# A two-layer decoder in one program: another cycle for the routing steps, another order at the first expert, and the mixers' first loads moved

## The chip, the cores and the metric

The kernel runs on one core of a Trainium2 chip. The metric is the device time of one execution in microseconds (us): the median of three runs was 3338.87 us (3336.57 to 3339.21). The profile is one execution more, and took 3336.63 us.

## The reference

The reference is a decoder of two layers with residual sums, on x of 8 sequences x 256 tokens x 512, all in float32. Each of its six blocks is fed the layer norm of x. Layer 0: causal attention with rotary positions, 16 heads and a window of 64; masked cross-attention to a context, with a layer norm of its own; then the mixture of experts that this change is about. Layer 1: a state-space mixer (Mamba2 form, chunks of 64), a channel attention to the context, and a feed-forward block of eight LoRA experts.

```python
logits = x @ gate_weight.T                       # x: 2048 tokens x 512, 64 experts
scores = softmax(logits)
gidx = top_k(scores.reshape(T, 8, 8).max(-1), 3)       # 3 of 8 groups
topk_w, topk_i = top_k(where(group mask, scores, 0), 6)    # 6 of 64 experts
pos = cumsum(one_hot(topk_i.flat)) at the chosen expert - 1     # place in the expert's list
slot = topk_i.flat * 192 + minimum(pos, 191)           # 192 slots per expert
buf = zeros(64 * 192, 512); buf[slot] = x[tok]
out = (silu(buf @ Wg.T) * (buf @ Wu.T)) @ Wd.T         # per expert, 704 wide
y = sum over 6 of out[slot] * topk_w
shared = silu(x @ Sg.T) * (x @ Su.T) @ Sd.T            # 704 wide
x = x + y + shared
```

The places in an expert's list run through all 2048 tokens in order, so the slots of a sequence need the counts of all sequences before it.

## The kernel before, in words

The program is a row of stages. In a stage each engine has its own instruction list, written out by hand in a `nc.Block()`: TensorE (`pe`), VectorE (`dve`), ScalarE (`act`), GpSimd (`pool`) and SyncE (`sp`), which issues most of the DMAs. They are ordered by counting semaphores alone (`wait_ge`, `then_inc`), and an engine executes its list strictly in order. At the end of a stage SP waits for all engines to be done (L145; each drains its queue at L129, GpSimd through `pool_link`) before the next stage's semaphores are used. Products in float32 are made of three products of a high and a low part (`..._hi`, `..._lo`): ScalarE writes the high part, VectorE or GpSimd subtracts it to get the low one.

The stages by the trace: attention up to about 821 us, the shared expert with the routing up to 1101, the 64 experts up to about 1904, the mixers of layer 1 up to about 2660, the LoRA experts to the end.

**Shared expert and routing** (`shared_expert`). The work is cut into 48 chunks g: 8 sequences s times six slices n of the 704 columns (`CHUNKS = NM * nseq`, `s, n = divmod(g, NM)`). In step g TensorE does `gate_up(g)` (L1175, three products of gate and of up for the slice), then `down(g - 2)` (L1190). ScalarE makes the tanh of the gate, VectorE the product `sact` (`gated`, `act_lo`), so a chunk's `down` comes two steps behind. After the last slice of a sequence VectorE adds the residual (`out`, `so`) and SP stores it as `mid`.

Between these products stands the routing of sequence r. Its steps and engines:

- `turn_rows(r, j)` on TensorE, for the two tiles j of 128 tokens; ScalarE's `turned` writes `h32` and `hT2`'s high part, GpSimd's `rows_lo` the low one (before: in slices 0 and 1 of sequence r - 1).
- `router(r)` on TensorE (L188, 64 columns of logits in PSUM bank 0), in slice 3 of sequence r - 1 (`router_step`), ahead of that step's `down`. It waits for `slot_ready` of sequence r - 1, since bank 0 also holds the counts and places.
- `negmax`, `exponentials` and `groups` in slice 4, `experts(r)` in slice 5 (VectorE, with ScalarE's exp; ends in `sel`, L1300).
- `counts(r)` on TensorE (L1153): the running counts as a product with a triangular matrix, in slice 0 of sequence r itself (`counts_step`), waits for `sel_ready`.
- `slots_of_experts(r)` and `slots(r)` on VectorE (`slots_steps`), in slices 1 and 2; for sequences 1 and 0, where the counts come in slice 1 or 2, both in one slice. They end in `slot_r` (L1326) and `tok_f` (L1327). SP stores weights and slots as `route_w` and `slots`.
- twelve scatters on GpSimd (L1042), from slice 3 on, two per slice, four per slice for the last sequence: each writes the token numbers of 128 slots to `slot_token`. `pool.wait_ge(sy["act_sh_ready"], g)` keeps them with the chunks.

For the last sequence `turn_last` and one reduction find the last token of each expert (slot 191); SP stores it. At the end of SP's list stand the waits for `so_out` of both buffers (one semaphore for `route_w`, `slots` and `mid`) and for the scatters.

**Experts.** Per expert SP loads indices and weights, GpSimd gathers 192 rows in two DMAs (`xg`, L1463), TensorE turns them (`turn_rows`, L1545), ScalarE copies them out (`xT_copy`, L1481) and VectorE makes the low part (`xT_lo`, L1605); then come the gate and up products (L1560), the activation on ScalarE and VectorE (L1500, L1633) and the `down` products. ScalarE's `hi_gu` and `hi_down` (L1490) and VectorE's `lo_gu` and `lo_down` split the weights. Ahead of the loop (`quads`) the first expert's list is written out: ScalarE does `hi_gu(0, 0)`, eight pad copies into the tails of `wd2` and `aT2` (L1520 to L1527, `epad_ready`), `hi_down(0, 0)`, `xT_copy(0, 0)`, `hi_gu(0, 1)`. TensorE waits for `ezero_ready` and for all eight pads, then turns the rows. VectorE does `lo_gu` twice, `lo_down` twice, then `xT_lo`. At the end of its list SP issues the loads of the mixers' weights (`next_weights`, semaphore `w3_in`): `w_in`, `small` and `w_mo`.

**Mixers.** For sequence s GpSimd gathers, in twelve indirect DMAs (`gather`, L1832), the experts' output rows into `yk`; VectorE adds them weighted to `xn` (`combine`, then the layer norm's statistics `mv`, L2278, and GpSimd's `norm`, L174), and TensorE turns the rows. `xn` (four buffers) is `mid`. SP's list begins with the loads of the routes of two sequences, of their `mid` rows, of the context and of two more sequences of `mid`; GpSimd waits for `routes_in` before its first gather, and its gathers of sequence 1 wait until VectorE has used the rows of sequence 0 (`yk_used`). VectorE does `combined_norm(0)` first, then the constants of the stage (`w3_in`, `norm_w`), then the loop over pairs of sequences.

Of the kernel before, what the change touches and what calls it, by code (L numbers as in the profile page):

```python
# [37 lines left out]
P = 128  # L38
# [48 lines left out]
hr_in0 hr_in1 xr_in0 xr_in1 so_out0 so_out1  # L87
# [836 lines left out]
def shared_expert(nc, sy, const, dr, held, nseq=NSEQ):  # L924
# [5 lines left out]
    with ExitStack() as ctx:  # L930
# [15 lines left out]
        hT2 = [parts(f"hrT{b}", [P, KC, S]) for b in range(2)]  # L946
# [34 lines left out]
        def counts_step(s):  # L981
            return max(0, 2 - s)

        def slots_steps(s):
            return (counts_step(s) + 1, max(2, counts_step(s) + 1))

        def router_step(s):
            return 4 if s == 0 else 3
# [9 lines left out]
        def _(sp):  # L998
# [9 lines left out]
            load_resid(1)  # L1008
            for s in range(nseq):
# [4 lines left out]
                sp.dma_start(dr["route_w"][s], etop[s % 2][:]).then_inc(sy[f"so_out{s % 2}"], 16)  # L1014
                sp.wait_ge(sy["slot_ready"], s + 1)
                sp.dma_start(dr["slots"][s], slot_r[s % 2][:]).then_inc(sy[f"so_out{s % 2}"], 16)
# [5 lines left out]
                sp.wait_ge(sy["shared_ready"], NT * (s + 1))  # L1022
                sp.dma_start(dr["mid"][s], o[s % 2][:]).then_inc(sy[f"so_out{s % 2}"], 16)
                if s + 2 < nseq:
                    load_resid(s + 2)
            for b in range(2):
                sp.wait_ge(sy[f"so_out{b}"], nseq // 2 * 48)
# [4 lines left out]
        def _(pool):  # L1032
            def rows_lo(s, j):
                pool.wait_ge(sy["hThi_ready"], NT * s + j + 1)
                cols = slice(j * P, (j + 1) * P)
                pool.tensor_tensor(hT2[s % 2][1][:, :, cols], h32[s % 2][:, :, cols],
                                   hT2[s % 2][0][:, :, cols].bitcast(F32), ALU.subtract).then_inc(sy["hTlo_ready"], 1)
# [27 lines left out]
            for g in range(CHUNKS):  # L1065
                s, n = divmod(g, NM)
                if n < NT and s + 1 < nseq:
                    rows_lo(s + 1, n)
                of = s if n >= 3 else s - 1
                if of >= 0:  # L1070
                    if n == 3:
                        pool.wait_ge(sy["slot_ready"], s + 1)
                    pool.wait_ge(sy["act_sh_ready"], g)
                    per = 4 if of == nseq - 1 else 2
                    for i in range(per):
                        scatter(of, per * (g - NM * of - 3) + i)
# [2036 lines left out]
```

## Time and profile before

| | |
|---|---|
| median of three runs | 3338.87 us (3336.57 to 3339.21) |
| the profiled execution | 3336.63 us |
| its span in the trace | 3334.9 us |
| mean granted clock of TensorE | 0.962 |

```profile
PE 3063.9 (92%) x22897; PEld 2472.5 (74%) x22897; DVE 2314.5 (69%) x4413; ACT 1598.0 (48%) x3648; POOL 805.0 (24%) x1000
PE   7999999997899699999999769889899889999999
PEclk9999999998999799999999979999999989999999
DMA  6324233321021677777777521311120032222222
```

The first line is the busy time of each engine, its share of the span and the number of its instructions: PE is TensorE's matmuls, PEld its loads of weights, DVE VectorE, ACT ScalarE, POOL GpSimd. The others cut the span into 40 slices of 83 us: busy tenths of TensorE, the clock granted to it in tenths of full speed, and how busy the DMA engines were. TensorE is nearly full everywhere but at the seams between the stages: slice 14 holds the seam ahead of the experts, slices 23 and 24 that ahead of the mixers.

### The profile page before, as it was taken

How to read it: one execution, taken by the hardware profiler on the slowest of the kernel's cores; microseconds unless marked ns; L12 is line 12 of the kernel's file. 1: busy time of each engine (PE TensorE's matmuls, PEld its weight loads, DVE VectorE, ACT ScalarE, POOL GpSimd, SP SyncE). 2: the span in 40 equal slices, each digit the busy share in tenths (PEclk: the TensorE clock that was granted, in tenths of full speed). 3: DMA queues.
4: the chain of work that ended last, by engine and by line, in shares of the span. 5: the costliest groups of instructions: out<-in, count | busy, mean ns of one | idle time of the engine just before them, and what ended most of it. 6: DMA issues, size and time to landing. Idle time of an engine off the chain costs nothing. (4 is left out here: it accounts for less than half of the span.)

```text
span 3334.9 us, 61560 instructions
## 1 busy us (share of the span) xinstructions
PE 3063.9 (92%) x22897; PEld 2472.5 (74%) x22897; DVE 2314.5 (69%) x4413; ACT 1598.0 (48%) x3648; POOL 805.0 (24%) x1000
## 2 busy tenths in 40 slices
PE   7999999997899699999999769889899889999999
PEld 5666666664888588888888646657576678888888
DVE  4655665564666588888888566868686767777776
ACT  3323333332221455555555336656575655555555
POOL 1221122121445211111111143432323012222222
PEclk9999999998999799999999979999999989999999
DMA  6324233321021677777777521311120032222222
GB/s 260 127 98 148 105 127 104 112 102 39 20 58 40 205 244 242 242 243 240 243 246 248 216 77 58 93 60 56 30 70 7 35 116 79 70 74 73 73 71 70
DMA packets 145099, 401.95 MB, mean 121 GB/s; under 512 B 39200, under 2 KB 48032, under 8 KB 131952
## 3 DMA queue, kind: packets, MB, share of 16 engines
q1 hardware_dynamic: 106448, 323.37, 28.6%
q0 software_dynamic: 18976, 50.45, 5.1%
q10 hardware_dynamic: 19456, 25.18, 2.2%
q8 instruction: 141, 2.31, 0.3%
q14 instruction: 78, 0.64, 0.1%
HBM read 344.16 MB, written 54.76 MB: 120 GB/s over the span
## 5 line engine op out<-in xcount | busy, mean ns | idle before, releaser
L1463 POOL DMA_INDIRECT xg<-normed_rows,idx x128 | 127.8, 998 | 643.3 <-PE psum L1545 589.5
L2631 POOL TENSOR_TENSOR mixf<-act 128x256 f32<-128x256 f32 x128 | 143.7, 1122 | 496.7 <-DVE act L2892 496.7
L174 POOL TENSOR_SCALAR ve<-mv 128x1 f32<-128x1 f32 x112 | 34.9, 312 | 841.6 <-DVE mv L780 575.0
L1560 PE MATMUL psum<-xT_hi,wgu_hi 128*128 128x192 f32 (+1 forms) x1536 | 228.4, 271 | 2.4 <-DVE xT_lo L1605 2.4
L1560 PE MATMUL psum<-xT_lo,wgu_hi 128*128 128x192 f32 (+1 forms) x1536 | 223.3, 268 | 0.0
L1560 PE MATMUL psum<-xT_hi,wgu_lo 128*128 128x192 f32 (+1 forms) x1536 | 222.5, 267 | 0.0
L1599 DVE TENSOR_TENSOR wgu_lo<-wgu,wgu_hi 128x1408 fp32r<-128x1408 f32 x128 | 202.6, 1624 | 22.9 <-ACT wgu_hi L1487 22.7
L1560 PEld LDWEIGHTS psum<-xT_hi,wgu_hi 128*128 128x128 f32 (+1 forms) x1536 | 190.6, 182 | 27.0 <-ACT wgu_hi L1487 21.6
L1500 ACT ACTIVATE eth<-psum 128x192 f32<-128x192 f32 (+1 forms) x192 | 63.4, 330 | 301.0 <-PE psum L1560 301.0
L2002 ACT ACTIVATE scratch<-psum,smin 128x512 f32<-128x512 f32 x256 | 173.9, 686 | 62.5 <-DVE smin L2392 60.3
L1560 PEld LDWEIGHTS psum<-xT_lo,wgu_hi 128*128 128x128 f32 (+1 forms) x1536 | 190.8, 183 | 0.0
L1560 PEld LDWEIGHTS psum<-xT_hi,wgu_lo 128*128 128x128 f32 (+1 forms) x1536 | 190.3, 182 | 0.0
L1487 ACT ACTIVATE wgu_hi<-wgu 128x1408 fp32r<-128x1408 f32 x128 | 169.6, 1382 | 27.1 <-DMA wd<-in_w_d_dram 27.1
L2392 DVE TENSOR_REDUCE smin<-psum 128x2 f32<-128x1024 f32 x128 | 155.3, 1216 | 34.1 <-PE psum L2156 33.3
L2892 DVE TENSOR_TENSOR act<-act,maskT 128x512 f32<-128x512 f32 x128 | 88.1, 689 | 117.7 <-ACT act L2669 117.6
L2166 PEld LDWEIGHTS psum<-ident,scratch 128*128 128x128 f32 x1024 | 108.9, 141 | 59.4 <-issue 38.2
L2166 PE MATMUL psum<-ident,scratch 128*128 128x128 f32 x1024 | 144.8, 281 | 8.1 <-DVE scratch L2399 4.9
L1633 DVE SCALAR_TENSOR_TENSOR eact<-eth,psum 128x192 f32<-128x192 f32 (+1 forms) x192 | 67.6, 352 | 110.8 <-ACT eth L1500 108.9
L2902 DVE TENSOR_TENSOR ca_lo<-act,ca_hi 128x512 fp32r<-128x512 f32 x128 | 134.4, 1050 | 12.5
L558 PE MATMUL psum<-hT_hi,w_slot 128*128 128x256 f32 x768 | 113.1, 291 | 12.2 <-ACT hT_hi L468 5.8
L1042 POOL DMA_INDIRECT slot_token<-tok_i,slot_w x96 | 99.4, 1035 | 80.4 <-DVE slot_r L1326 31.1
L902 DVE TENSOR_SCALAR arena<-psum,hi 128x512 f32<-128x512 f32 x128 | 87.2, 744 | 43.8 <-PE psum L672 43.8
(427 smaller groups left out, 8665.0 us busy)
## 6 DMA issues: line engine op xcount, KB each, us to landing
wgu<-in_w_gu_dram SPq DMA_DIRECT2D x64, 1408.0 KB, 6.1
w_slot<-w_split SPq DMA_DIRECT2D x21, 2048.0 KB, 8.8
wd<-in_w_d_dram SPq DMA_DIRECT2D x64, 512.0 KB, 8.7
w_raw<-in_w_dram SPq DMA_DIRECT2D x128, 256.0 KB, 2.6
expert_out<-yo ACTq DMA_DIRECT2D x64, 256.0 KB, 5.2
w_slot<-w_split SPq DMA_DIRECT2D x28, 512.0 KB, 5.1
wd<-in_w_d_dram SPq DMA_DIRECT2D x64, 192.0 KB, 9.1
w_split<-w_slot SPq DMA_DIRECT2D x4, 2048.0 KB, 9.5
```

Source lines behind the costliest of these rows:

```text
L558: ins = pe.matmul(out, lhs_of(lp, kc), rhs_of(rp, kc), start=(m == 0 and kc == 0), stop=(m == 2 and kc == KC - 1))
L1042: pool.indirect_dma_start(out=dr["slot_token"], out_offset=bass.IndirectOffsetOnAxis(ap=slot_w[s % 2][:, j, k:k + 1], axis=0), in_=tok_i[s ...
L1463: pool.indirect_dma_start(out=xg[b][0:w, t, :], out_offset=None, in_=rows, in_offset=bass.IndirectOffsetOnAxis(ap=idx[b][0:w, t:t + 1], ax ...
L1487: act.activation(wgu2[b][0][:, gu], wgu[b][:, gu], ACT.Copy).then_inc(sy["wgu_hi"], 1)
L1560: ins = pe.matmul(bank(2 + m)[0:w, gu * CAP:(gu + 1) * CAP], wgu2[b][wp][:, gu, kc, m0:m0 + w], xT2[b][xp][:, kc, :], start=(i == 0 and kc ...
L1599: dve.tensor_tensor(wgu2[b][1][:, gu], wgu[b][:, gu], wgu2[b][0][:, gu].bitcast(F32), ALU.subtract).then_inc(sy["wgu_lo"], 1)
L2002: act.activation(prob[:, q % 4, k, :], bank_pair(2 * (q % 2))[:, k, :], ACT.Exp, bias=smin[b][:, n, k:k + 1], scale=-1.0, accum_out=ssum[b ...
L2166: ins = pe.transpose(bank(4 + k)[:, mc * P:(mc + 1) * P], prob[:, q % 4, k, mc * P:(mc + 1) * P], ident)
L2392: dve.tensor_reduce(smin[(q // PAIRS) % 2][:, q % PAIRS, :], bank_pair(2 * (q % 2)), AX.X, ALU.min).then_inc(sy["smin_ready"], 1)
L2631: pool.tensor_tensor(mixf[:, g % LAG, :], act2[:, g % LAG, 0, :], act2[:, g % LAG, 1, :], ALU.add).then_inc(sy["f_mix"], 1)
L2892: dve.tensor_tensor(act2[:, g % LAG], act2[:, g % LAG], maskT[(g // FC) % 2][:, 2:4, :], ALU.mult).then_inc(sy["f_ca"], 1)
L2902: dve.tensor_tensor(ca2[1][:, g % LAG], act2[:, g % LAG], ca2[0][:, g % LAG].bitcast(F32), ALU.subtract).then_inc(sy["f_ca_lo"], 1)
```

## The change

The routing runs in a cycle of its own, of five chunks in place of six (`CYCLE = 5`), so it gets ahead of the chunks of its sequence: rows of sequence r are turned in chunks 5r - 4 and 5r - 3, `router(r)` stands in chunk 5r - 1 behind that chunk's `down`, `negmax` to `groups` in 5r, `experts` in 5r + 1, `counts` in 5r + 2, `slots_of_experts` and `slots` together in 5r + 3, and the twelve scatters in 5r + 4 to 5r + 7, three in each. The turned rows get a third buffer, the stores of routes a semaphore apart from `so_out` (`rt_out`), and SP stores `mid` one turn later. In the experts' stage the first `xT_copy` goes ahead of the pads, the first `turn_rows` ahead of the wait for them, and `xT_lo` ahead of `lo_down`. The mixers' first two routes and first four sequences of `mid` are loaded behind the mixers' weights at the end of the experts' list of SP; the gathers of sequence 1 go to `scratch` and `y[1]`, with semaphores of their own, and wait for nothing; GpSimd's `norm(0)` stands behind 18 gathers; and VectorE's `combined_norm(0)` behind the constants.

```diff
+        CYCLE = 5
+        def in_cycle(g, phase, first=0):
+            r, at = divmod(g - phase, CYCLE)
+            return r if at == 0 and first <= r < nseq else None
+        def turned_in_chunk(g):
+            for j in range(NT):
+                r = in_cycle(g, j - CYCLE + 1, 1)
+                if r is not None:
+                    return r, j
+            return None
...
-        hT2 = [parts(f"hrT{b}", [P, KC, S]) for b in range(2)]
+        hT2 = [parts(f"hrT{b}", [P, KC, S]) for b in range(3)]
...
@@ SP: route_w and slots go to rt_out, mid one turn later
-                sp.wait_ge(sy["shared_ready"], NT * (s + 1))
-                sp.dma_start(dr["mid"][s], o[s % 2][:]).then_inc(sy[f"so_out{s % 2}"], 16)
-                if s + 2 < nseq:
-                    load_resid(s + 2)
+                if s >= 1:
+                    store_rows(s - 1)
+            store_rows(nseq - 1)
...
@@ GpSimd
-                if n < NT and s + 1 < nseq:
-                    rows_lo(s + 1, n)
-                of = s if n >= 3 else s - 1
-                if of >= 0:
-                    if n == 3:
-                        pool.wait_ge(sy["slot_ready"], s + 1)
-                    pool.wait_ge(sy["act_sh_ready"], g)
-                    per = 4 if of == nseq - 1 else 2
-                    for i in range(per):
-                        scatter(of, per * (g - NM * of - 3) + i)
+                if turned_in_chunk(g):
+                    rows_lo(*turned_in_chunk(g))
+                for i in range(4):
+                    r = in_cycle(g, 4 + i)
+                    if r is not None:
+                        pool.wait_ge(sy["slot_ready"], r + 1)
+                        pool.wait_ge(sy["act_sh_ready"], g)
+                        for k in range(3):
+                            scatter(r, 3 * i + k)
...
@@ TensorE
-                if s + 1 < nseq:
-                    if n < NT:
-                        turn_rows(s + 1, n)
-                    if n == router_step(s):
-                        router(s + 1)
+                if turned_in_chunk(g):
+                    turn_rows(*turned_in_chunk(g))
                 if g >= 2:
                     down(g - 2)
-                if s < nseq and n == counts_step(s):
-                    counts(s)
-                if s == nseq - 1 and n == 3:
+                r = in_cycle(g, -1, 1)
+                if r is not None:
+                    router(r)
+                r = in_cycle(g, 2)
+                if r is not None:
+                    counts(r)
+                if g == CYCLE * nseq:
                     turn_last()
...
@@ VectorE: negmax and groups at in_cycle(g, 0), experts at in_cycle(g, 1)
-                if s < nseq and n == slots_steps(s)[0]:
-                    slots_of_experts(s)
-                if s < nseq and n == slots_steps(s)[1]:
-                    slots(s)
+                r = in_cycle(g, 3)
+                if r is not None:
+                    slots_of_experts(r)
+                    slots(r)
...
@@ experts, ScalarE
             hi_gu(0, 0)
+            xT_copy(0, 0)
             act.wait_ge(sy["ezero_ready"], 7)
...
             hi_down(0, 0)
-            xT_copy(0, 0)
             hi_gu(0, 1)
...
@@ experts, TensorE
+            turn_rows(0, 0, 0, True)
             pe.wait_ge(sy["epad_ready"], 8)
-            turn_rows(0, 0, 0, True)
...
@@ experts, VectorE
+            xT_lo(0, 0)
             for part in range(2):
                 lo_down(0, 0, part, 0)
-            xT_lo(0, 0)
...
@@ mixers' tiles and loads
+    for b in range(2):
+        loads += [(tiles[f"slots{b}"][:], dr["slots"][b]), (tiles[f"wk{b}"][:], dr["route_w"][b])]
+    for s in range(4):
+        loads.append((tiles[f"xn{s}"][:], dr["mid"][s]))
...
@@ mixers, SP
-            load_routes(0)
-            load_rows(0)
-            load_routes(1)
-            load_rows(1)
             load_cx(0)
-            load_rows(2)
-            load_rows(3)
...
@@ mixers, GpSimd
-                if n == 0:
-                    pool.wait_ge(sy["routes_in"], 64 * (s // 2 + 1))
-                if s and k == 0:
+                if n == 0 and s < 2:
+                    pool.wait_ge(sy["w3_in"], W3A)
+                elif n == 0:
+                    pool.wait_ge(sy["routes_in"], 64 * (s // 2))
+                if s >= 2 and k == 0:
                     pool.wait_ge(sy["yk_used"], GATHERS * (s - 1) + TOPK * (j + 1))
...
-            for s in range(2):
-                for n in range(GATHERS):
-                    gather(s, n)
-                norm(s, norm1(s))
+            for n in range(2 * GATHERS):
+                gather(n // GATHERS, n % GATHERS)
+                if n == GATHERS + TOPK - 1:
+                    norm(0, norm1(0))
+            norm(1, norm1(1))
...
@@ mixers, VectorE
-            combined_norm(0)
             dve.wait_ge(sy["w3_in"], W3A)
...
+            combined_norm(0)
```

## Rows read from the trace of the kernel before

**Rows 1.** Stretch, length; busy PE, PEld, DVE, ACT, POOL; granted clock; DMA share; GB/s.

```profile
829.00:1088.40 259.40, 244.64 (x1691) 225.16 (x1690) 168.57 (x483) 60.21 (x168) 125.30 (x115) 0.96 0.14 38
1088.40:1101.70 13.30, 0.08 (x1) 0.00 (x0) 0.81 (x2) 0.00 (x0) 2.77 (x3) 0.55 0.11 40
1101.70:1122.70 21.00, 1.94 (x8) 1.57 (x8) 9.06 (x14) 9.74 (x16) 6.20 (x5) 0.50 0.74 244
1122.70:1899.60 776.90, 776.41 (x6456) 687.25 (x6456) 627.02 (x1146) 423.84 (x695) 121.59 (x123) 1.00 0.73 241
1899.60:1935.00 35.40, 0.00 (x0) 0.00 (x0) 11.11 (x17) 1.08 (x3) 14.63 (x21) 0.53 0.58 205
```

**Rows 2.** Waits of TensorE, 820 to 1090 us: total us, times, longest.

```profile
PE psum L188 <- DVE slot_r L1326: 11.8, 7, 3.2
...
PE psum L1153 <- DVE sel L1300: 2.1, 1, 2.1
```

**Rows 3.** Timeline of TensorE, 849 to 857 us: start, duration, instruction, [idle before].

```profile
849.22 0.40 PE L1190 MATMUL psum<-sd_hi,sact_hi 128*128 128x512 f32 x1
...
850.61 0.64 PE L1175 MATMUL psum<-hrT_hi,sg_hi 128*128 128x256 f32 x4
...
853.00 0.64 PE L1175 MATMUL psum<-hrT_hi,su_lo 128*128 128x256 f32 x4
...
856.80 3.01 PE L188 MATMUL psum<-w_gate,hrT 128*128 128x64 f32 x16 [3.16 <-DVE slot_r L1326]
```

**Rows 4.** Timeline of VectorE at the end of the slots of sequence 0.

```profile
856.48 0.17 DVE L1326 CAST slot_r<-over 128x16 int32<-128x16 f32 x1
```

**Rows 5.** Busy time by stretch, behind the wait for `sel` and behind the first for `slot_r`.

```profile
845.00:853.00 8.00, 7.87 (x60) 7.62 (x61) 7.34 (x18) 0.69 (x2) 3.50 (x3) 1.00 0.01 2
857.00:865.00 8.00, 8.00 (x38) 7.31 (x38) 1.46 (x5) 0.70 (x4) 5.91 (x6) 0.57 0.03 1
```

**Rows 6.** Attention stage: a wait of TensorE on the timeline, and that stretch's busy time.

```profile
38.62 3.53 PE L558 MATMUL psum<-w_slot,hT_hi 128*128 128x512 f32 x8 [2.70 <-DVE w_slot L823]
...
38.00:42.00 4.00, 3.38 (x9) 2.68 (x10) 0.56 (x1) 0.00 (x0) 0.00 (x0) 0.57 0.98 416
```

**Rows 7.** End of the shared expert's stage: SP's waits, the drains (ns, starts), the last scatter.

```profile
SPq L145 <- POOLq L129: 9.0, 1, 9.0
...
SPq L145 <- DMA mid<-so: 2.3, 1, 2.3
...
L129 POOLq DRAIN  x2: 679/4331/7983, 815.5 to 1093.0; - x2
...
1090.80 0.98 POOL L1042 DMA_INDIRECT slot_token<-tok_i,slot_w  x1 [0.30 <-issue]
```

**Rows 8.** First expert: timeline of three engines, and a DMA issued at 1106.44.

```profile
1115.10 0.63 ACT L1524 ACTIVATE wd_hi<-wd 32x512 fp32r<-32x512 f32 x1
...
1118.31 1.06 ACT L1490 ACTIVATE wd_hi<-wd 128x1024 fp32r<-128x1024 f32 x1
...
1118.38 1.94 PE L1545 MATMUL psum<-ident,xg 128*128 128x128 f32 x8 [29.91 <-ACT aT_lo L1526]
...
1120.36 0.87 ACT L1481 ACTIVATE xT_hi<-psum 128x384 fp32r<-128x384 f32 x2 [0.48 <-PE psum L1545]
...
1128.15 0.35 DVE L1633 SCALAR_TENSOR_TENSOR eact<-eth,psum 128x192 f32<-128x192 f32 x1 [2.42 <-ACT eth L1500]
...
xg<-normed_rows,idx POOLq DMA_INDIRECT x1, 9.8
```

**Rows 9.** Mixers' start: a load issued at 1862 us, and GpSimd's timeline.

```profile
w_mo<-in_w_mo_dram SPq DMA_DIRECT2D x1, 1024.0 KB, 17.8
...
1909.98 0.96 POOL L1832 DMA_INDIRECT yk<-expert_out,slots  x1 [4.42 <-DMA wk<-route_w]
...
1923.86 1.28 POOL L1832 DMA_INDIRECT yk<-expert_out,slots  x1 [0.30 <-issue]
...
1933.41 0.24 POOL L174 TENSOR_SCALAR ve<-mv 128x1 f32<-128x1 f32 x1 [8.27 <-DVE mv L2278]
```

## What the change will do to the time

> **What bounds the kernel now.** I read the table of stages first [rows 1]: it gives the busy time of each engine in each stretch. In the shared expert's stage TensorE is busy for 244.6 of 259.4 us, and in the experts' stage for 776.4 of 776.9 us, so there only TensorE's own waits and its clock can be saved. Between the stages stand stretches in which TensorE does almost nothing: 13.3 us after the shared expert, 21.0 us ahead of the first expert's products (1.9 us busy), and 35.4 us ahead of the mixers. The change touches the shared expert's stage and all three of these stretches. Next come the waits of TensorE in that stage [rows 2]: 11.8 us in seven waits of the router product for `slot_ready`, and one of 2.1 us for `sel_ready`. Then each such place in order of time [rows 3 to 9]. The chain of waits says little here, since it ends long after.
>
> The change has four parts on the path. Call them A (routing cycle), B (end of that stage), C (first expert) and D (start of the mixers).
>
> **A. Routing in a cycle of five chunks.** A chunk on TensorE is `gate_up` and `down`. From the starts in [rows 3] `down` takes 850.61 - 849.22 = 1.39 us, `gate_up` from 850.61 to 853.64, some 3.0 us there and 2.87 us at its usual pace (24 matmuls at the same spacing of 0.12 us). The work of TensorE is the same as before: no product is added or taken away. What changes is where `router(r)` stands. For r = 1 and 2 VectorE did all of `slots_of_experts` and `slots` in one chunk's step already, and TensorE waited 3.16 us for it [rows 3]; a second such wait of 3.17 us follows 32 us later. For r = 3 to 7 the two halves lay in two steps, and each wait was (11.8 - 2 x 3.16) / 5 = 1.1 us [rows 2]. After the change all seven have the one-step form of r = 1, but `router` comes behind `down(g - 2)`, not ahead of it. TensorE thus arrives 1.39 us later, and the wait is 3.16 - 1.39 = 1.77 us. VectorE's side stays: the `slot_r` that releases it starts at 856.48 [rows 4], 7.3 us after the `gate_up` of that chunk ended, against 1.39 + 3.03 + 1.39 = 5.8 us on TensorE. Waits: 7 x 1.77 = 12.4 us instead of 11.8, so +0.6 us.
>
> The larger item is the clock. After the wait of 3.16 us the granted clock falls from full speed (2.4 GHz) to half (1.2 GHz): its mean over the next eight microseconds is 0.57 [rows 5], a loss of 8 x 0.43 = 3.4 us, and the second wait of this length costs the same 3.4 us. The five waits of 1.1 us are followed by none. The nearest row to a wait of 1.77 us is the one of 2.1 us for `sel_ready` [rows 2], which ends at 845.1 and is followed by a clock of 1.00 [rows 5]; the nearest on the other side is 2.70 us in the attention stage, where the mean is 0.57 over four microseconds [rows 6]. I take no fall at 1.77 us: -6.9 us. Bounds of A: -8.0 (waits 0.2 us shorter) and, if all seven waits cost a fall, +17.5. Taken: +0.6 - 6.9 = -6.3 us.
>
> What else A moves: `turn_rows(1, 0)` leaves chunk 0 for chunk 1, and `turn_rows(1, 1)` goes from 1 to 2; both starts of weights and VectorE hide it. `experts(r)` ends 5.3 us after its `gate_up`, and `counts(r)` comes 1.39 + 2.87 + 1.39 = 5.65 us after it and 1.0 more where two turns lie between: no wait, though with 0.4 us to spare for r = 7. Without that cover it costs up to 0.5 us each. GpSimd gets 12 scatters at 1.27 us and two `rows_lo` at 1.3 us in four chunks, 17.9 us of some 22. On SP's queue the store of `mid` moves one turn back; its buffers are wanted over five chunks later, so it costs nothing. The third `hT2` is what lets the rows be turned early.
>
> **B. End of the stage.** Before, the routing of the last sequence came in chunks 42 to 44 and its twelve scatters lie past the last product: the last starts at 1090.80, GpSimd's DRAIN starts at 1093.0 and takes 7.98 us, and SP waits 9.0 us for it after the store of `mid` has landed (2.3 us) [rows 7]. Afterwards the slots are ready in chunk 38 and the scatters go in chunks 39 to 42. Chunks 43 to 47 and the two last `down` are some 5 x 4.27 + 2 x 1.39 = 24 us, so scatters and drain (1.0 + 8.0 us, and landing) end ahead of the last product. What is late next is the store of `mid`, unchanged. Gain: the 9.0 us. Bounds: -9.5 and 0 (the drain may belong to the stage's end and not to the scatters).
>
> **C. First expert's rows ahead of the pads.** This looks like a gain of the 3.2 us that the eight pad copies take (1115.10 to 1118.31), since TensorE turns the rows at 1118.38, right behind them [rows 8]. But it is one queue: ScalarE now waits for the turned rows before it writes the pads. The second half of the rows is asked for at 1106.44 and takes 9.8 us [rows 8], so it lands at 1116.2; turning takes 2.0 us (to 1118.3), `xT_copy` 0.87 us, the pads 3.2 us: 1122.4. `pe.wait_ge(epad_ready, 8)` still stands ahead of all products, so the first product starts at 1122.4 instead of 1122.73. `hi_down` (1.6 us) follows, to 1124.0, `lo_down` on VectorE (1.9 us) to 1125.9 and `lo_gu(1)` (3.15 us) to 1129.1. Before, VectorE gated the first product at 1128.15 [rows 8]. It is 1.0 us later now and has no slack there: TensorE ends that expert 0.8 us later. The steady state is TensorE's, so this stays. C: +0.8 us. Bounds: -2.0 (rows land 3 us sooner) and +2.5 (rows land 2 us later).
>
> **D. Start of the mixers.** The routes and four sequences of `mid` are loaded by SP behind the mixers' weights, in the experts' stage. That is 2.1 MB in eight more issues at 1862 us; the last weights land 17.8 us after their issue [rows 9], at about 1880, and the mixers start at 1904, so the loads are hidden with some 15 us to spare. GpSimd waited 4.42 us for the routes until 1909.98 [rows 9]; it now goes on at 1905.6. The twelve gathers are a row of 1.26 us each, the last starts at 1923.86, and VectorE works on the second tile as they land; everything up to the first turned rows at 1935 hangs on them. So -4.4 us. Moving VectorE's constants ahead of `combined_norm(0)` fills idle time, and where they stood (3.4 us) VectorE waited 2.2 us more for TensorE: nothing. The twelve gathers of sequence 1 no longer wait for `yk`, but sequence 1 is combined only behind `convolved(0)`, at 1958: nothing either. Behind six of them GpSimd's norm of sequence 0 is now queued. It would be reached at 1905.6 + 18 x 1.26 = 1928.3, and is wanted at 1933.41 - 4.4 = 1929.0 [rows 9]: 0.7 us to spare. Bounds: -5.4 (less traffic beside the gathers) and -1.9. The lower gain is that of gathers as slow as the last one of before, 1.28 us instead of 0.95 [rows 9], for eight or ten of the eighteen.
>
> The Trainium skill has a rule for this in "SBUF — State Buffer", section "Who interferes with whom": a VectorE instruction with two SBUF inputs contends with GpSimd instructions that read SBUF, and the later one waits. The combine is such an instruction, and the last gather's 1.28 us agrees in direction, at 0.33 us and not a whole instruction.
>
> **Sum.** -6.3 - 9.0 + 0.8 - 4.4 = -18.9 us. The profiled execution took 3336.63 us and so would take 3317.7. The median of the runs shown lies 2.2 us above it, so I predict 3320.0 us.
>
> **Rivals.**
> 1. *The clock falls at every router wait* (the other side). Place: TensorE ahead of `router(r)`, seven times. VectorE's one-step routing makes each wait 2.7 us rather than 1.77, and each pays the fall of a long wait. Price: 7 x 2.7 - 11.8 = +7.1, 7 x 3.4 - 6.9 = +16.9, A = +24.0 and the sum +11.4: 3350.3 us, slower. It decides from somewhere between 2.1 and 2.7 us of idle time. For it: one of the five VectorE steps might be longer by 0.4 us. Against it: the 2.1 us row. Chance 0.07.
> The Trainium skill, "TensorE: Matmul & The Clock Gate", section "HAM oscillation — how this bites in real kernels", says that a loop with an idle gap in each turn pays the slow clock in each turn; its gap is longer than the 1.77 us here, and the rows with 2.1 and 3.16 us fit it.
> 2. *The drain isn't hidden*: it is a property of leaving the stage after many scatters. For it: at the end of the attention stage, with no scatters, it takes 0.68 us [rows 7], which fits both readings. B = 0: 3329.0 us. Chance 0.12.
> 3. *The mixers' lead is lost* to GpSimd's queue. D = -1.9: 3322.5 us. Chance 0.11.
> 4. *Two falls of the clock stay*, since the wait of 2.1 us comes just before. A = +0.6: 3326.9 us. Chance 0.08.
> My forecast has the remaining 0.62.
>
> **Numbers.** The range is 3315.5 to 3330.5 us: from the upper gains of B, C and D (-22.3, less 1 us of spread) to rival 2 with a little loss beside it. Some 0.2% (6.7 us) is what a measurement of this kernel can tell from no change. Rival 1 is slower by 0.34%. Everything else is faster by more than 0.2%, less some chance that two rivals meet. Faster 0.88, same 0.05, slower 0.07.
>
> **What would show it.** A: seven waits of 1.6 to 2.1 us of the router product for `slot_r`, and a granted clock of 1.00 from 850 us on to the end of the stage. B: SP's wait for GpSimd's drain is gone, and the next stage starts 3 us after the last `so`. C: ScalarE idle some 3 us ahead of `xT_hi`; first product 0 to 0.5 us earlier and the steady state 0.8 us later, each counted from the stage's start. D: first gather within 2 us of the mixers' start, first turned rows 26.7 us after it instead of 31.0. It would be wrong if a clock below 1 follows the waits, or if the drain stands in the same place.

## The result, and the profile after

The changed kernel takes 3333.51 us (median of 22 runs, 3323.48 to 3337.58) where the kernel before takes 3338.39 us (22 runs, 3334.75 to 3343.21): a ratio of 0.9984, with an interval of 0.9978 to 0.9990. That is 4.9 us, where 18.9 us were forecast, and the time lies outside the range. Forecast faster, it is faster by less than the 0.2% that I had called telling.

The stages after, in the order and the columns of [rows 1]:

```profile
830.03:1093.25 263.22, 247.94 (x1691) 228.44 (x1690) 172.03 (x483) 60.05 (x168) 129.64 (x117) 0.95 0.14 38
1093.25:1097.78 4.53, 0.00 (x1) 0.00 (x0) 0.73 (x2) 0.00 (x0) 0.00 (x0) 0.62 0.29 116
1097.78:1119.09 21.31, 1.94 (x8) 1.57 (x8) 7.30 (x11) 6.72 (x13) 5.34 (x5) 0.50 0.73 240
1119.09:1897.10 778.01, 777.35 (x6456) 688.14 (x6456) 628.44 (x1148) 426.62 (x699) 120.04 (x124) 1.00 0.73 243
1897.10:1929.50 32.40, 0.00 (x1) 0.03 (x1) 14.18 (x25) 0.97 (x3) 22.46 (x27) 0.54 0.68 204
```

The seam behind the shared expert has shrunk from 13.3 to 4.5 us, the one ahead of the mixers by 3 us (the first stretch in which TensorE does nothing there is 32.6 us where it was 35.4). But the shared expert's stage has not. From its first turned rows to its last product it took 266.85 us before (821.63 to 1088.48) and takes 270.59 now (822.66 to 1093.25). The two profiled executions, whose spans differ by 4.6 us (3334.9 and 3330.3), add up as follows:

| part | forecast | measured | from |
|---|---|---|---|
| ahead of the stage, untouched | 0 | +1.0 | 821.63, 822.66 |
| A, first turned rows to last product | -6.3 | +3.7 | 266.85, 270.59 |
| B, last product to next stage's first load | -9.0 | -8.7 | 13.24, 4.53 |
| C, that load to the mixers' start | +0.8 | +1.3 | 802.29, 803.58 |
| D, mixers' start to first turned rows | -4.4 | -2.9 | 31.03, 28.14 |
| behind the mixers' first turned rows, untouched | 0 | +0.9 | 1399.9, 1400.8 |

So 10.0 us are missing in A and 1.5 us in D. In A it is not the waits. TensorE's waits in the stage after, as in [rows 2]:

```profile
PE psum L188 <- DVE slot_r L1337: 12.6, 7, 2.0
PE psum L1163 <- DVE sel L1311: 2.1, 1, 2.1
```

Seven waits, 12.6 us, where 12.4 were forecast. The clock makes the difference. Here are the seven waits on TensorE's timeline, and under them, in the same order, the busy table from each wait's start to nine microseconds behind its end; the granted clock is the third number from the right:

```profile
857.45 1.94 PE L188 MATMUL psum<-w_gate,hrT 128*128 128x64 f32 x14 [1.87 <-DVE slot_r L1337]
886.42 1.75 PE L188 MATMUL psum<-w_gate,hrT 128*128 128x64 f32 x14 [1.87 <-DVE slot_r L1337]
913.42 1.75 PE L188 MATMUL psum<-w_gate,hrT 128*128 128x64 f32 x14 [1.47 <-DVE slot_r L1337]
940.44 2.92 PE L188 MATMUL psum<-w_gate,hrT 128*128 128x64 f32 x14 [1.65 <-DVE slot_r L1337]
970.52 1.90 PE L188 MATMUL psum<-w_gate,hrT 128*128 128x64 f32 x12 [1.88 <-DVE slot_r L1337]
1001.12 2.21 PE L188 MATMUL psum<-w_gate,hrT 128*128 128x64 f32 x14 [2.00 <-DVE slot_r L1337]
1030.24 1.97 PE L188 MATMUL psum<-w_gate,hrT 128*128 128x64 f32 x16 [1.88 <-DVE slot_r L1337]
```

```profile
855.58:866.45 10.87, 9.00 (x60) 8.77 (x60) 5.61 (x21) 1.39 (x6) 6.20 (x6) 0.84 0.16 49
884.55:895.42 10.87, 9.00 (x72) 8.72 (x73) 6.61 (x28) 1.39 (x6) 5.83 (x6) 1.00 0.47 148
911.95:922.42 10.47, 9.00 (x71) 8.78 (x72) 7.42 (x30) 1.39 (x6) 5.80 (x6) 1.00 0.55 151
938.79:949.44 10.65, 9.00 (x46) 8.83 (x47) 5.04 (x16) 1.39 (x6) 5.83 (x6) 0.68 0.53 145
968.64:979.52 10.88, 9.00 (x45) 8.63 (x46) 3.82 (x14) 1.39 (x6) 5.82 (x6) 0.69 0.02 1
999.12:1010.12 11.00, 9.00 (x59) 8.78 (x59) 5.33 (x20) 1.38 (x6) 5.90 (x6) 0.84 0.03 3
1028.36:1039.24 10.88, 9.01 (x72) 8.77 (x72) 6.78 (x28) 1.38 (x6) 6.52 (x7) 1.00 0.02 1
```

Behind waits 1, 4, 5 and 6 the clock falls to half (1.2 GHz) for some time. Length times (1 - clock) is what it costs: 1.7, 3.4, 3.4 and 1.8 us, 10.3 together, against 6.8 us before (two falls of 3.4 us; the first is in [rows 5]). The forecast had put it at nothing. Busy time alone misleads here: TensorE is busy for all nine microseconds either way, but it gets through 46 matmuls in one stretch and 72 in another.

### The profile page after: what moved, and what is told of

It is laid out like the page before. It is cut to its first block and busy times, and to the rows that moved or that the text cites. A ratio compares the mean times of both kernels' runs of the same rounds, so it can differ in the third digit from the quotient of the medians.

```text
span 3330.3 us, 61582 instructions
## 1 busy us (share of the span) xinstructions
PE 3071.3 (92%) x22897; PEld 2479.2 (74%) x22897; DVE 2317.9 (70%) x4413; ACT 1596.5 (48%) x3648; POOL 805.7 (24%) x1000
```

## The experiments

Each kernel was run beside the kernel before, which took 3377.36 us in the first set of runs (e1 to e4), 3376.91 in the second (e5 to e8), 3338.03 in the third (e9 to e12), 3378.09 in the fourth (e13 to e15) and 3380.59 in the last. Where it is near 3378 the mixers' stage, which lies behind all that is studied here, takes 31 to 48 us more in the traces; so each time is read against the before of its own set, and each part from its own stretch of the trace. "Stage" is first turned rows to last product of the shared expert's stage, "clock" what slow clock costs in it from 834 us on; a "fall" is a drop of the granted clock to half. A "gap" is idle time of TensorE that the profile puts down to "issue", that is, to nothing it shows.

**e1: C and D alone** (the shared expert's stage as before).

> The changed kernel with the shared expert's stage of before (parts C and D alone). In the profile after, C cost 1.05 us (31.75 instead of 30.70 us from the stage's first load to the second turn of rows) and D gave 2.9 (28.14 instead of 31.03 us to the mixers' first turned rows). Theory 1 (what was missing lies in the routing stage, in its clock): 1.9 us under before, the stage itself 266.9 us from the first turned rows to the last product as before, two falls of the clock, the 9.0 us wait for the drain back. Theory 2 (C and D together cost more than they give, in stages behind them): at or above the time of before.

3373.39 us, ratio 0.9992 (0.9983 to 1.0001), 4.0 us under before. The two falls behind 3.2 us waits are there, the five waits of 1.1 us have none. The stage took 274.7 us, not 266.9: TensorE stood still for 5.6 us ahead of the last products, with 3.4 us of clock behind it. The profile calls this a gap, but TensorE lacked an operand. ScalarE starts the tanh of the last chunk only 5.4 us after the last gate and up product (which ends at 1084.07); in the first profile of before it starts as that product ends, at 1083.57. Why ScalarE is late the profile doesn't show ("remote" is its word for a release whose sender it doesn't find).

```profile
1089.43 0.38 ACT L1124 ACTIVATE sth<-psum 64x256 f32<-64x256 f32 x1 [8.64 <-remote]
```

With the seam behind it the stage took 280.2 us, as in the first profile of before (280.1), so this lost time cost nothing. Theory 2 has no support, though the interval just includes no change. Theory 1's 1.9 us lies within the interval too.

**e2, e7: take the wait away.**

```diff
-                    pe.wait_ge(sy["slot_ready"], s)
+                    pe.wait_ge(sy["place_ready"], s)
```

> The changed kernel with one word changed: router(r) waits for place_ready, after which VectorE reads bank 0 no more, and not for slot_ready, 3.5 us later. Theory 1 (the waits of 1.5 to 2.0 us are what costs, half of them by a fall of the clock): 12.6 us of waits and 10.2 us of slow clock go, stage 270.6 - 22.8 = 247.8 us, 22.8 us under the changed kernel. Rival (the stage is longer for another reason, late operands in the cycle of five): the wait of 12.6 us turns into waits for sel, sact_lo or hrT_lo, and the gain is below 10 us.

3377.04 us, ratio 0.9997 (0.9986 to 1.0007); the stage 280.0 us where theory 1 had 247.8, clock 15.4 us. The rival holds: the router waits no more, but in its place stands the wait for `sel`. Two of these waits (1.67 and 1.76 us) are followed by a fall, 5.1 us together; the other 10.2 us of clock lie beside 5.1 us of gaps in two late chunks (see e16).

```profile
PE psum L1163 <- DVE sel L1311: 12.3, 8, 2.1
```

In this cycle TensorE reaches the routing products before VectorE's routing chain does: with the router released earlier, `counts`, the next of them, waits. So e7 also gives `counts` the time that it needs, behind `gate_up` of the next chunk:

```diff
                     gate_up(g)
+                r = in_cycle(g, 3)
+                if r is not None:
+                    counts(r)
...
-                r = in_cycle(g, 2)
-                if r is not None:
-                    counts(r)
```

> The changed kernel with router waiting for place_ready, and counts(r) moved from chunk 5r + 2 to behind gate_up of chunk 5r + 3. Theory 1b (VectorE's routing chain sets the cycle: with the wait for the slots gone the wait for sel came in its place, 1.4 to 2.1 us each): now neither is waited for, no falls but the first ones, stage 248 to 252 us instead of 270.6 and 280, and the kernel 18 to 23 us under the changed one. Rival (VectorE lacks time over the five chunks altogether): waits for sact or negmax appear, stage over 262 us.

3359.40 us, ratio 0.9946 (0.9930 to 0.9961), 22.5 us under the changed kernel (e5), within the 18 to 23 expected. The stage is 259.4 us where the changed kernel took 284.2 in the same set; neither `slot_r` nor `sel` is waited for, and `sact_lo` five times, 3.3 us. It misses the expected 248 to 252 us by 7.4; that is in 4.8 us of gaps and the 5.1 us of clock beside them (see e16).

**e3: the longer wait** (`router(r)` ahead of `down(g - 2)`).

> The changed kernel with router(r) ahead of its chunk's down, so that each wait is 1.87 + 1.39 = 3.26 us. Theory 1 (the longer the wait, the likelier the fall; at 3.2 us it always falls): waits 22.8 us (+10.2), seven falls of 3.4 us (23.8 instead of 10.2), stage 294 us, 24 us over the changed kernel. Rival (the falls are tied to something else than the length of the wait, as the place in the stage): the same number of falls as after, four, and 10 us over it.

3395.43 us, ratio 1.0053 (1.0040 to 1.0066). Waits of 22.0 us, seven falls of seven, as theory 1 had it. They cost 20.5 us and not 23.8, since a fall costs 1.7 to 5.1 us; with 5.1 us more of clock beside gaps in a late chunk the stage is 300.4 us, where 294 were expected.

**e4: the one word in the kernel before.**

> The kernel before with router waiting for place_ready in place of slot_ready, all else as it was. Theory 1: waits of 11.8 us and two falls of the clock (7 us) go: 18.8 us under before, stage 248 us. Rival: the waits are moved to sel_ready or to the chunks' own operands, gain under 8 us.

3363.68 us, ratio 0.9959 (0.9946 to 0.9972): 13.7 us under before, more than the whole change gives, though short of theory 1's 18.8. No fall is left in the routing; two more waits for `sel` came, 3.1 us. The stage is 259.3 us and not 248: TensorE stands still for 7.0 us ahead of the last products, again behind a late tanh of ScalarE (6.8 us after the last gate and up product), and the 3.4 us of clock lie there.

**e5, e6: the changed kernel and the kernel before again**, for their traces.

> The changed kernel itself once more, to see its waits and its clock in a second profile on the chip of this call. Theory 1 (a wait of 1.5 to 2.0 us is followed by a fall of the clock in some executions and places, not in others): again seven waits of about 1.8 us, another set of them followed by falls, 7 to 14 us of clock lost in the stage, and the gain over before again well under the 18.9 us forecast. Rival (the falls of the first profile are fixed to those four waits): the same four.

3381.86 us, ratio 1.0011 (1.0002 to 1.0020): here the changed kernel is the slower one. Waits of 12.8 us as ever, falls behind waits 1, 4, 5, 6 and now 7: my rival, the same places, holds better than the theory that they are drawn anew each time. But the stage takes 284.2 us, 13.6 more than in the first profile: 3.4 us of gaps near 1077 us, 5.1 us of clock beside them, and 5.1 us more behind waits 6 and 7 (20.5 us of clock in all).

> The kernel before itself, for a profile on the same chip as the others of this call. Theory 1: two falls of the clock of 3.4 us behind the waits of 3.2 us, and 13.2 us from the last product to the next stage's first load. If TensorE's idle 5.6 to 7.0 us ahead of the last product, seen in the stage of before in two experiments, belongs to the twelve scatters late in that stage, it stands here too and the 13.2 us are shorter by as much.

3375.21 us (one run). There are two falls, behind the two waits of 3.2 us. Ahead of the last products TensorE waits 4.9 us, again behind ScalarE's tanh of the last chunk (4.6 us after the last gate and up product), and SP's wait for the drain is 5.9 us shorter than in [rows 7]:

```profile
PE psum L1190 <- DVE sact_lo L1242: 4.9, 1, 4.9
...
SPq L145 <- POOLq L129: 3.1, 1, 3.1
```

Stage and seam together are 280.5 us (273.2 + 7.3), as in the first profile (266.85 + 13.24 = 280.1): before, the lost time lies in the shadow of GpSimd's scatters and drain. As expected, the seam is shorter by what the stage is longer.

**e8, e9: the pads.** e8 moves TensorE's wait for the pads to the first `down`; e9, on top of e7, puts ScalarE's pads back ahead of `xT_copy` and leaves the rest of C as changed.

> The changed kernel with TensorE's wait for the eight pads moved from ahead of the first products to ahead of the first down. Theory (the pads behind xT_copy are what holds the first product): first product 19.2 us after the stage's first load instead of 21.3, second turn of rows 29.6 instead of 31.75: 2.1 us under the changed kernel. Rival (VectorE's lo_gu of expert 1, 3.15 us, holds the first down): first product earlier, second down not, no gain in the steady state.

3378.14 us, ratio 1.0008 (0.9998 to 1.0018). The second turn of rows comes at 29.0 instead of 31.5 us, but then `down` waits four times, 2.4 us, for VectorE's `aT_lo` (e5: once, 0.4 us), and the stretch to the mixers' start is 804.6 us against 803.0 in e5. That is the rival: VectorE's queue holds the first `down`, and nothing is gained in the steady state.

> The kernel with router on place_ready and counts in chunk 5r + 3, and ScalarE's eight pads back ahead of xT_copy, where it sits idle 3.5 us until the rows are turned (TensorE still turns them ahead of its wait for the pads). Theory (the loss of C is the pads' 3.2 us behind xT_copy, which delay hi_down, lo_down and lo_gu of expert 1 on VectorE): first product 19.2 us after the stage's first load, and from that load to the mixers' start 800 to 801 us instead of the 803 to 804 us of the changed kernel and the 802.3 us of before. Over the same kernel without this edit: 3 us less. Rival (the moves' order on TensorE is the loss): 803 us.

3307.57 us (4 runs, 3300.83 to 3308.56), ratio 0.9909 (0.9893 to 0.9924): 30.5 us under before, the lowest ratio of all, in a set without gaps. Load to mixers' start 800.6 us, as expected; the stage 246.8 us without any fall. The rows that answer to [rows 2] are gone but for

```profile
PE psum L1200 <- DVE sact_lo L1253: 2.2, 1, 2.2
```

**e10, e16, e17: no scatters.** The scatters and the waits for them are left out; every expert then computes the same row.

> The changed kernel without the 96 scatters of token numbers and the waits for them (the lists of the experts stay zero, so every expert computes the same row). Theory H (the holes of TensorE that no wait explains, 3 to 7 us near the end of the stage, and some of the fall of the clock, come from the scatters beside them): no such hole, waits for slot_r as before at 1.5 to 2.0 us, and the stage 5 to 12 us shorter than that of the changed kernel on the same chip (271 us on one chip, 284 on another). Rival (the holes are late instructions of TensorE that have nothing to do with the scatters): the same holes, and the stage unchanged.

3333.24 us, ratio 0.9987 (0.9978 to 0.9996), stage 273.9 us, the same seven waits, and falls behind 1, 4, 5, 6 and 7; but no gaps stood in the third set in any kernel (e12 neither), so this told nothing of them. It told that falls need no scatters, and it told of B: GpSimd's drain (min/median/max of two, ns; the long one was 7983 [rows 7]) is short without scatters:

```profile
L129 POOLq DRAIN  x2: 132/406/681, 816.2 to 1066.9; - x2
```

> The changed kernel without its 96 scatters once more (every expert then computes the same row), beside the changed kernel with them. Where the runs of before take 3377 us and not 3338, TensorE's matmuls of one chunk near the end of the stage come with gaps of 0.4 to 1.5 us that no wait explains (3.4 us in e5_after, with 5.1 us of slow clock). Theory H (these gaps come from the scatters beside them): gone without scatters, kept with them. Rival (late instructions, whatever GpSimd does): in both. If neither shows them, before takes 3338 us here and the question stays open.

> The changed kernel itself beside e16. If before takes 3377 us here: gaps of about 3.4 us and 5 us of slow clock in one chunk near the end of the stage, stage 284 us. If before takes 3338 us: none, stage 271 us, falls at waits 1, 4, 5 and 6.

e17: 3379.72 us, ratio 1.0000 (0.9989 to 1.0012), with the gaps; e16: 3370.16 us, ratio 0.9973 (0.9957 to 0.9989), without. First some rows of the chunk with the gaps on the timeline of e17 and its busy table, then the busy table of e16, in which that chunk lies at about 1070 us:

```profile
1072.21 0.64 PE L1185 MATMUL psum<-hrT_hi,su_lo 128*128 128x256 f32 x4
...
1074.82 0.38 PE L1185 MATMUL psum<-hrT_hi,sg_hi 128*128 128x256 f32 x1 [0.23 <-issue]
...
1076.24 0.28 PE L1185 MATMUL psum<-hrT_lo,sg_hi 128*128 128x256 f32 x1 [0.70 <-issue]
...
1078.36 0.37 PE L1185 MATMUL psum<-hrT_hi,sg_lo 128*128 128x256 f32 x1 [1.12 <-issue]
...
1080.57 0.39 ACT L1134 ACTIVATE sth<-psum 128x256 f32<-128x256 f32 x1 [10.08 <-remote]
...
1073.00:1083.00 10.00, 6.72 (x31) 5.77 (x30) 1.17 (x3) 1.10 (x4) 4.45 (x5) 0.76 0.02 0
```

```profile
1070.00:1080.00 10.00, 10.00 (x68) 8.92 (x67) 4.61 (x11) 1.58 (x5) 0.00 (x0) 1.00 0.13 52
```

31 matmuls in ten microseconds against 68. Theory H holds: the stage is 283.9 us with scatters and 273.7 without. Of the 10.2 us, 3.3 are gaps, 5.1 the clock beside them, and 1.7 a longer fall behind wait 7. It isn't TensorE alone. ScalarE's tanh of the chunk before (the ACT row) starts 7.7 us after that chunk's last product (the first row, to 1072.85), and the gaps end as it starts. In the first profiles and in the third set no tanh from 850 us on is over 0.6 us late; in every kernel with scatters of the other sets one is late by 4.6 to 7.8 us, beside the gaps or the stillness, and in e16 none is. What passes between the scatters and these engines is open. The late matmuls' own operands come from earlier chunks, and the profile shows nothing that they wait for. For the kernel before (e1, e4, e6) the tie to the scatters is likely but not shown, since no run leaves them out there.

**e11, e14: shorter waits.** A semaphore on VectorE's second write of `over` (e11) or on its write of `slot_w` (e14) releases the router.

> The changed kernel with router waiting for VectorE's second write of over, 0.7 us ahead of slot_r: seven waits of about 1.1 us (0.8 to 1.4) in place of 1.8. Theory 1 (the length of the wait decides whether the clock can fall behind it; at 1.1 us the kernel before showed none): waits 8 us, at most one fall, stage 258 to 262 us. Rival (any wait will do, or the falls have another cause): four to five falls as after, stage only 5 us shorter.

3321.41 us, ratio 0.9947 (0.9933 to 0.9960): waits of 0.9 to 1.4 us (8.3 together), one fall of 1.7 us, stage 258.6 us, as theory 1 had it.

> The changed kernel with router waiting for slot_w, 0.5 us ahead of slot_r: seven waits of about 1.4 us (1.0 to 1.6). Theory 1 (the longer, the likelier a fall): two to four falls, between the one of the waits of 0.9 to 1.4 us and the four to five of those of 1.5 to 2.0; stage 260 to 266 us. Rival (a sharp bound near 1.5 us): one fall, stage 260.

3377.69 us, ratio 0.9999 (0.9988 to 1.0010): waits of 1.1 to 1.6 us, three falls (1.7, 3.4, 1.7 us), within the two to four expected. The stage missed its 260 to 266 us: it took 279.4, with 5.7 us of gaps and 6.8 us of clock beside them.

**e12: without D.**

> The changed kernel with the mixers of before (A, B and C alone). By the profile after, D is worth 2.9 us up to the first turned rows. Theory: this kernel 2.9 us over the changed one, 31.0 us to the first turned rows. Rival (D's gathers and loads take it back further on, in the mixers' stage): equal to the changed one or under it.

3335.89 us, ratio 0.9993 (0.9984 to 1.0002) against 0.9984 of the changed kernel: 3.0 us, though the intervals overlap. First turned rows 30.8 us after the mixers' start, near the 31.0 expected. So D seems to keep what it gains; the times alone don't prove it.

**e13: the same waits, 5 us later and more** (24 more transposes ahead of the stage).

> The changed kernel with 24 more transposes of TensorE ahead of its first turned rows in the shared expert's stage (about 6 us that shift all that follows; their result is overwritten). In five profiles of the cycle of five with seven waits of 1.5 to 2.0 us the waits 1, 4, 5 and 6 were followed by a fall of the clock each time, 7 in three of them, 2 and 3 never, although 2 is as long as 1. Theory P (which of these waits is followed is decided by when they come): another set falls. Rival (by the place in the program, or by the length to a tenth of a microsecond): the same set.

3392.64 us, ratio 1.0042 (1.0027 to 1.0057). The first two router waits come 5.1 us later than after, the others, behind more falls, 8 to 11 us later. All seven are followed by a fall, 2 and 3 among them, at the same lengths as after:

```profile
891.50 2.74 PE L188 MATMUL psum<-w_gate,hrT 128*128 128x64 f32 x14 [1.87 <-DVE slot_r L1339]
...
921.61 2.61 PE L188 MATMUL psum<-w_gate,hrT 128*128 128x64 f32 x16 [1.48 <-DVE slot_r L1339]
```

```profile
890.00:901.00 11.00, 9.50 (x49) 9.22 (x50) 2.90 (x12) 1.06 (x6) 5.83 (x6) 0.69 0.45 146
920.00:931.00 11.00, 9.53 (x62) 9.16 (x62) 6.51 (x26) 1.39 (x6) 5.82 (x6) 0.84 0.50 144
```

The wait for `sel`, on whose 2.1 us the prediction rested, changes sides as well. In the other fifteen profiles that have it, it is 2.06 to 2.13 us long, ends between 844 and 847 us, and no fall follows. Here it is shorter, and a fall of 1.7 us follows (a wait of 1.38 us for `sact_lo` ends 3.5 us ahead of it):

```profile
849.29 0.43 PE L1163 MATMUL psum<-sel,tri_lt 128*128 128x64 f32 x2 [1.89 <-DVE sel L1313]
...
849.00:858.00 9.00, 8.71 (x55) 8.45 (x56) 6.91 (x16) 0.69 (x2) 3.65 (x3) 0.81 0.01 2
```

So a wait of this length may or may not cost the clock, and what e13 changed is when it comes. What in the time decides stays open.

**e15: `norm(0)` right behind its twelve gathers**, on top of e9.

> The kernel of e9_pads_in_gap with GpSimd's norm of sequence 0 right behind the twelve gathers of that sequence, no longer behind six of the next. Theory (the gather ahead of norm holds it 0.4 us): first turned rows 27.1 to 27.5 us after the mixers' start instead of 27.5 to 27.9, no more; the time within 1 us of e9_pads_in_gap, 30 us under before. Rival (the gathers of sequence 1 are late then, and hold combined_norm(1)): 3 us or more over it.

3356.46 us, ratio 0.9937 (0.9923 to 0.9951), 21.6 us under before, with gaps as in e17 (5.5 us, and 5.1 us of clock) in its stage. First turned rows 27.4 us after the mixers' start, as expected, but 27.5 in e9. From the twelfth gather to the first turned rows 10.95 us instead of 11.43: 0.5 us, most of it taken back by slower gathers. Whether it is the better version can't be told across sets.

Router waits for VectorE's slots by length, over all profiles in which they stood:

| length, us | kernels | waits | followed by a fall |
|---|---|---|---|
| 1.08 to 1.10 | before, e1, e6 | 15 | 0 |
| 0.86 to 1.37 | e11 | 7 | 1 |
| 1.12 to 1.59 | e14 | 7 | 3 |
| 1.47 to 2.02 | after, e5, e8, e10, e12, e16, e17 | 49 | 33 |
| 1.48 to 2.00 | e13 | 7 | 7 |
| 2.81 to 3.30 | before, e1, e6, e3 | 13 | 13 |

The table holds router waits alone. Beside them stand the fifteen waits for `sel` of 2.1 us without a fall.

## Why the prediction was wrong

**A is the step that failed, by its second term.** "I take no fall at 1.77 us: -6.9 us" rested on one row, the 2.1 us wait for `sel` with a clock of 1.00 behind it, and took it for a property of the length. The clock term was +3.5 us in its place (10.3 instead of 6.8), which is 10.4 us off, as much as is missing in A. The row was true and showed one of two outcomes: the four middle rows of the table above have 44 falls in 70 waits of 0.9 to 2.0 us, and e13 shows that the same waits change sides when they come some 5 us later. That the seven waits got four falls, and not two or seven, was luck of their times. Rival 4 (two falls stay) was nearer than the forecast, and rival 1's premise, "it decides from somewhere between 2.1 and 2.7 us", was wrong as well: the longer the wait, the more often a fall follows, but between 1.2 and 2.1 us the length alone doesn't decide. The bound of +17.5 for A did hold the outcome, but the range was not built on it. Its lower end was also mis-summed: -6.3 - 9.5 - 2.0 - 5.4 is -23.2, not -22.3, and A with waits 0.2 us shorter is -7.7, not -8.0; neither bears on the miss. The Trainium skill's "TensorE: Matmul & The Clock Gate", section "HAM oscillation — how this bites in real kernels", warned of a loop with a gap in each turn; I had set it aside because its gap is longer than 1.77 us. The traces agree with it in kind, and at shorter gaps than that loop's: of seven turns with a gap of 1.5 to 2.0 us, four to seven pay.

**The waits** were right: seven of 1.47 to 2.00 us, 12.6 us. What was not asked is whether the router needs `slot_ready` at all. In all seven turns VectorE's chain is the last to end, before and after, so the reordering left the waits at what they were in sum (11.8 and 12.6 us). e4 and e7 show what lay in the wait itself.

**B** was right, -8.7 us for -9.0. After, the drain takes the same 7.98 us, but it starts at 1073.62, well ahead of the last product. That it belongs to the scatters and not to the stage's end, the doubt behind B's bound of 0, is shown by e10. What I did not see is that it covered something: the gaps that the scatters put into TensorE's last chunks, or the late tanh beside them, cost nothing before, since GpSimd ended later anyway. They cost the changed kernel 3.4 us and 5.1 us of clock in e5. With the 5.1 us more behind waits 6 and 7 that is why the ratio goes from 0.9984 to 1.0011 and 1.0000.

**C** had the right mechanism and a size off by 0.5 us: the first product comes 21.31 us after the stage's first load instead of 21.01, forecast 0 to 0.5 earlier, for the rows are turned 10.4 us behind the second gather's issue and not 9.8. e8 shows that the delay sits in VectorE's queue and e9 that the pads cause it.

**D** gave 2.9 of 4.4 us, by the mechanism of its lower bound (slower gathers, on which rival 3's price was built). Counted from the mixers' start, the first gather is 4.3 us earlier, as forecast, but the twelfth only 2.9 us. GpSimd's gathers (start, duration) and VectorE's combine beside them:

```profile
1912.14 0.95 POOL L1853 DMA_INDIRECT yk<-expert_out,slots  x1 [0.30 <-issue]
1913.40 1.43 POOL L1853 DMA_INDIRECT yk<-expert_out,slots  x1 [0.31 <-issue]
1915.13 1.27 POOL L1853 DMA_INDIRECT yk<-expert_out,slots  x1 [0.30 <-issue]
1916.71 1.27 POOL L1853 DMA_INDIRECT yk<-expert_out,slots  x1 [0.30 <-issue]
1918.28 0.95 POOL L1853 DMA_INDIRECT yk<-expert_out,slots  x1 [0.30 <-issue]
...
1913.25 4.69 DVE L2296 SCALAR_TENSOR_TENSOR xn<-yk,wk,xn 128x512 f32<-128x512 f32 x6 [6.93 <-DMA yk<-expert_out,slots]
```

A gather takes 1.27 to 1.43 us while VectorE combines (1913.25 to 1917.94) and 0.95 otherwise. VectorE starts the first tile's combine 3.6 us after the sixth gather's start, where it was 5.7 us before, and so combines beside more of the second tile's gathers. Before, it did so beside the last two, and only the last was slow, 1.28 us [rows 9]. The Trainium skill's "SBUF — State Buffer", section "Who interferes with whom", names this pair, and the trace agrees in kind, at 0.3 to 0.5 us a gather and not a whole instruction. The sum is 0.26 us (1.21 us beside the scaling of `w_mo`) + 0.48 + 0.32 + 0.32 = 1.4 us, which is the shortfall. GpSimd's queue, which rival 3 names, holds `norm(0)` 0.5 us (e15 against e9). From the twelfth gather to the first turned rows it is 11.2 us both before and after, so this took nothing from D.

## What to carry to other kernels

A wait of TensorE is to be priced with the clock behind it, and one row of a wait without a fall is no proof for its length: count all waits of that size and carry both outcomes into the range. When a schedule is shortened, ask first what the waiting instruction truly needs. `place_ready` already tells that bank 0 has been read, and `slot_ready` came 3.7 us after it in the changed kernel (3.6 or 6.1 us before); the one word gave 13.7 us in e4, where the whole change gave 4.9. A stretch that hides behind a long drain becomes visible once the drain is gone, so look at what lies in its shadow before you count the gain.

## What the runs showed of the hardware

- GpSimd's drain at the end of the shared expert's stage took 7.98 us in all seventeen profiles with scatters, and 0.13 us in the two without (e10, e16).
- A fall of the clock behind a wait of TensorE cost 1.7 or 3.4 us, once 5.1 us (e3). The same seven waits, the first of them 5.1 us later, had all seven falls instead of four or five (e13); the fifteen waits for `sel` of 2.1 us at 844 to 847 us had none.
- Scatters of 128 single words, one each 1.28 us, can go with TensorE's matmuls at less than half their rate (31 in ten microseconds, 68 without scatters), where the profile shows nothing that they wait for, and with a ScalarE that starts a tanh up to 7.8 us late. This was so in four of five sets of runs and never in the third, nor in the first profiles.
